# Moving one elementwise product from GpSimd to VectorE in a four-stage kernel whose engines run from hand-ordered tables

## The chip, the cores and the metric

One NeuronCore of one Trainium2 chip runs the whole program. The metric is the device time of one execution in microseconds (us), as the median of several runs. The profile is of one such execution.

## The reference, cut to what matters

The input is 32 images of 128 channels by 32x32 pixels, which is 128 x 1024 numbers per image, in float32. Four blocks follow each other:

```
x = whitening(x)            # 4x4 covariance over all images, Cholesky, one 1x1 mix
x = mamba(x) + x            # per image: norm, W_in, causal conv, silu -> xc ; silu(z)
                            #   delta = softplus(W_dt dt + b)
                            #   h[n] = h[n] * exp(delta * A[n]) + (delta * xc) * B[n]     n = 0..15
                            #   y = sum_n h[n] * C[n] + xc * Dp ; out = W_out (y * silu(z))
x = gamma * attention(x) + x  # 1024 x 1024 softmax per image
x = batchnorm(conv(attention2(x))) + x   # a second 1024 x 1024 softmax per image
```

The change is about the factor `delta * xc` of the recurrence. The kernel calls it `du`.

## The kernel before, in words

The first 150 us or so read all images once for the whitening statistics. The last 110 us or so apply the batch norm. Between them stands the main part: 32 images, each in two chunks of 512 positions (`c` = 0, 1), each chunk in 16 rows (`r`). In row `r` of chunk `c` the kernel does recurrence step `k = 16c + r`, which handles two of the 16 states for one half `h` of the 256 inner channels. So rows 0 to 7 are half 0 and rows 8 to 15 are half 1. The same rows carry pieces of other work: the front of the next chunk (norm, conv, gates, step sizes), and eight tiles of one of the two attentions of an earlier image.

What each engine does within a row, and in which order, is written out in four tables of words (`ORDER_PE`, `ORDER_DVE`, `ORDER_ACT`, `ORDER_POOL`), one string for each of the 16 rows. Each engine runs its own words in that order without overtaking, and waits on semaphores of the others. The words that matter here are these.

- On VectorE (DVE), `dbu` (`spread_inputs`, L554) multiplies the B row by `psU` into PSUM, twice. `scan0` and `scan1` (L567) run the recurrence for the two states into `hs`. `max` (L587) takes the row maximum of an attention tile, `recip` (L581) a reciprocal, and `attend` (L599 and L602, or L606 and L609) scales the attention output. `gate` (L573) forms `y * silu(z)` into `g`, and `normed` (L539) multiplies `xcen` by `rstd`, both in SBUF. `inputs` (L545) copies `du` of the next half into the PSUM bank `psU`.
- On GpSimd (POOL), `prod` (`products`) multiplies `hs` by the C rows (L370), adds the pair of states (L376) and in every second row adds two pairs (L380). In rows of chunk 0 it also copies the last column of the state (L374). `delta0` and `delta1` (`step_size`) finish the step sizes of the next chunk (L356) and multiply them by `xc` into `du` (L361).
- On ScalarE (ACT), `decay` (L752) makes `exp(delta * A)` for the step after, `exp` (L794) the softmax numerators, `copya` and `copyb` (L760) bring transposed tiles out of PSUM, `spread` (L801) the reciprocal sums, and `sp` and `ln` make the softplus parts.
- On TensorE (PE), `energy` makes an attention tile, `turna` and `turnb` transpose it, `weigha` and `weighb` multiply it by the values, `inner0` and `inner1` are the conv products, which wait for `normed`, and `add` sums `prod` results into `psY`.

`hs` has three slots and `pa` four, so VectorE can be at most two steps ahead of GpSimd. The buffer `g` is the same memory as `du`. A max of an attention tile follows its `energy`, the `exp` follows the max, and the next `energy` follows that `exp`.

Of the kernel before, what the change touches and what calls it, by code (L numbers as in the profile page):

```python
# [15 lines left out]
NCH = L // CH  # L16
BCR = 2 * NS
PAIRS = NS // 2
# [13 lines left out]
def build(nc, x, w0, b0, ln_w, ln_b, w_in, conv_w, conv_b, w_x, w_dt, b_dt, a_log, dp, w_out,  # L32
          w_q, b_q, w_k, b_k, w_v, b_v, gam, th_w, ph_w, cv_w, bn_g, bn_b, out):
    fp32, bf16 = mybir.dt.float32, mybir.dt.bfloat16
    ALU = mybir.AluOpType
# [3 lines left out]
    with ctx:  # L39
# [56 lines left out]
        rstd = sb("rstd", [128, CH])  # L96
# [4 lines left out]
        xc = sb("xc", [128, NH, L])  # L101
# [3 lines left out]
        delta = sb("delta", [128, NH, L])  # L105
        du = sb("du", [128, NH, L])
# [45 lines left out]
        S = {}  # L152
# [15 lines left out]
        for k in range(SLOTS):  # L168
# [7 lines left out]
            xi_mm=2 * NCH, xi_ok=2 * NCH, z_mm=2 * NCH, z_ok=2 * NCH, xc_ok=2 * NCH,  # L176
            dbl_mm=NCH, rows_ok=NCH,
            dpre_mm=2 * NCH, sp_abs=2 * NCH, sp_relu=2 * NCH, sp_exp=2 * NCH, sp_ln=2 * NCH,
            delta_ok=2 * NCH, du_ok=2 * NCH,

            u_ok=2 * NCH, dbu_ok=2 * STEPS, da_ok=2 * STEPS, h_ok=2 * STEPS,
            hlast_ok=STEPS // 2, prod=STEPS, pair=STEPS, quad=STEPS // 2, quad_mm=STEPS // 2, g_ok=2 * NCH,
# [9 lines left out]
        def wait(eng, name, b, k):  # L192

            value = b * PER[name] + k
            if isinstance(value, int) and value <= 0:
                return
            eng.wait_ge(S[name], value)

        def at(eng, name, value):
# [33 lines left out]
        ORDER_PE = [  # L233
            "centre variance",
            "energy7 add turna6 weigha2 turnb6",
            "weighb2 resx turna7 residual",
            "turnb7 weigha3 weighb3 query add",
            "",
            "inner0 add inner1",
            "key energy0",  # L240
            "add",
            "values energy1 turna0",
            "gates1 turnb0 skip0 add energy2 gates0",
            "rows turna1 turnb1",
            "energy3 steps0 add",
            "weigha0 steps1 weighb0 turna2 energy4 turnb2 turna3 skip1 turnb3",
            "add",
            "energy5 turna4 weigha1 turnb4 weighb1",
            "turna5 energy6 turnb5 add",
        ]  # L250

        ORDER_DVE = [
            "dbu scan0 scan1 max6",
            "dbu scan0 attend1 scan1 gate1",
            "dbu max7 scan0 scan1",
            "dbu recip3 attend2 scan0 normed scan1",
            "dbu scan0 scan1 attend3",
            "dbu scan0 scan1",
            "dbu scan0 scan1",
            "dbu scan0 inputs scan1 max0",  # L260
            "dbu scan0 scan1 max1",
            "dbu scan0 scan1",
            "dbu scan0 max2 scan1",
            "dbu gate0 scan0 scan1 max3",
            "dbu recip0 scan0 recip1 scan1",
            "dbu scan0 scan1 max4 attend0",
            "dbu scan0 scan1 max5",
            "dbu scan0 inputs recip2 scan1",
        ]

        ORDER_ACT = [
            "decay0 decay1 centre exp6",
            "decay0 spread1 decay1 rstd copya6",
            "exp7 copyb6 spread2 decay0 copya7 decay1",
            "residual copyb7 decay0 spread3 decay1",
            "decay0 decay1",
            "xi0 decay0 decay1 query",
            "decay0 decay1",
            "key decay0 decay1",
            "decay0 xi1 decay1 exp0 value",  # L280
            "decay0 copya0 exp1 decay1 copyb0 silu0 silu1 z1 z0",
            "table decay0 copya1 exp2 decay1 rows",
            "copyb1 decay0 decay1 sp0 exp3",
            "decay0 sp1 decay1 copya2",
            "decay0 ln0 copyb2 decay1 spread0 copya3 exp4",
            "decay0 copyb3 ln1 decay1 copya4 exp5 copyb4",
            "copya5 decay0 decay1 copyb5",
        ]

# [11 lines left out]
            "prod",  # L301
            "prod",
            "prod",
            "prod delta0",
            "prod",
            "prod delta1",
        ]

        def parts(word):
# [12 lines left out]
        def cols(c):  # L322
            return slice(c * CH, (c + 1) * CH)
# [3 lines left out]
        with nc.Block() as block:  # L327


            @block.gpsimd  # L330
            def _(pool):
                n = [0]

                def link(ins):
                    n[0] += 1
                    ins.then_inc(S["consts_made"], 1)
                    pool.wait_ge(S["consts_made"], n[0])

                link(pool.memset(ident[:, :], 0.0))
                link(pool.affine_select(out=ident[:, :], in_=ident[:, :], compare_op=ALU.not_equal, fill=1.0,  # L340
                                        base=0, pattern=[[-1, 128]], channel_multiplier=1))
                link(pool.memset(mask32[:, :], 0.0))
                for q in range(4):
                    link(pool.affine_select(out=mask32[:, :], in_=mask32[:, :], compare_op=ALU.not_equal, fill=1.0,
                                            base=-32 * q, pattern=[[-1, 32]], channel_multiplier=1))
                link(pool.memset(avg[:, :], 1.0 / C))
                link(pool.tensor_tensor(cent[:, :], ident[:, :], avg[:, :], ALU.subtract))
                link(pool.memset(xn[:, 0:KC - 1], 0.0))
                mark["consts"] = n[0]

                def step_size(fb, fc, h):
                    i = 2 * fc + h + 1
                    wait(pool, "sp_relu", fb, i)
                    wait(pool, "sp_ln", fb, i)

                    pool.tensor_tensor(delta[:, h, cols(fc)], delta[:, h, cols(fc)], sp_l[:, h, :], ALU.add  # L356
                                       ).then_inc(S["delta_ok"], 1)
                    wait(pool, "delta_ok", fb, i)
                    wait(pool, "xc_ok", fb, i)
                    wait(pool, "x1_mm", fb - 1, fc + 1)  # L360
                    pool.tensor_tensor(du[:, h, cols(fc)], delta[:, h, cols(fc)], xc[:, h, cols(fc)], ALU.mult  # L361
                                       ).then_inc(S["du_ok"], 1)

                def products(b, k):
                    sl, slot = (b * STEPS + k) % HRING, k % RING
                    h, q = divmod(k % NS, PAIRS)
                    wait(pool, "h_ok", b, 2 * k + 2)
                    wait(pool, "quad_mm", b, k // 2 - 1)
                    at(pool, f"rl{slot}", (b * (STEPS // RING) + k // RING + 1) * 16)
                    pool.tensor_tensor(pa[:, k % PROD, :, :], hs[:, sl, :, :], rows_all[:, slot, 2:4, :], ALU.mult  # L370
                                       ).then_inc(S["prod"], 1)
                    if k < NS:

                        pool.tensor_copy(hlast[:, h, 2 * q:2 * q + 2], hs[:, sl, :, CH - 1]).then_inc(S["hlast_ok"], 1)  # L374
                    wait(pool, "prod", b, k + 1)
                    pool.tensor_tensor(pa[:, k % PROD, 0, :], pa[:, k % PROD, 0, :], pa[:, k % PROD, 1, :], ALU.add  # L376
                                       ).then_inc(S["pair"], 1)
                    if k % 2:
                        wait(pool, "pair", b, k + 1)
                        pool.tensor_tensor(pa[:, k % PROD, 0, :], pa[:, (k - 1) % PROD, 0, :], pa[:, k % PROD, 0, :], ALU.add  # L380
                                           ).then_inc(S["quad"], 1)

                def image(b, scan, more):
                    for c in range(NCH):
                        for r in range(NS):
                            front_of = front_part(b, c, scan, more)
                            for word in ORDER_POOL[r].split():
                                what, n = parts(word)
                                if what == "delta" and front_of:
                                    step_size(*front_of, n)  # L390
                                if what == "prod" and scan:
                                    products(b, NS * c + r)

                for h in range(NH):
                    step_size(0, 0, h)
                image(0, True, True)
                image(1, True, True)
                for b in range(2, NB - 1):
                    image(b, True, True)
                image(NB - 1, True, False)  # L400
# [3 lines left out]
            def _(dve):  # L404
# [135 lines left out]

                def inputs(b, k):
                    ch, h = divmod(k // PAIRS, NH)
                    wait(dve, "du_ok", b, k // PAIRS + 1)
                    wait(dve, "dbu_ok", b, 2 * k)
                    dve.tensor_copy(psU[:, :], du[:, h, cols(ch)]).then_inc(S["u_ok"], 1)  # L545

                def spread_inputs(b, k):
                    slot = k % RING
# [21 lines left out]

                def gate(b, ch, h):
                    wait(dve, "quad_mm", b, (NS * ch + PAIRS * (h + 1)) // 2)
                    dve.tensor_tensor(g[:, h, cols(ch)], psY[:, :], sz[:, h, cols(ch)], ALU.mult  # L573
                                      ).then_inc(S["g_ok"], 1)

# [750 lines left out]
```

## Time and profile before

| | us |
|---|---|
| median of three runs | 5245.92 |
| lowest and highest | 5242.39, 5246.16 |
| the profiled execution, its own time | 5247.66 |
| its span | 5245.8 |

| engine | busy us | share of the span |
|---|---|---|
| PE | 4574.1 | 87% |
| DVE | 4798.9 | 91% |
| ACT | 3722.0 | 71% |
| POOL | 4717.1 | 90% |

1.86 us of the profiled execution lie outside its span. The granted TensorE clock is full in the whole of the main part. Busy shares are means over setup, main part and end. An engine that shows no idle time over an image of the main part can set its period. What the others wait for has to be read in the main part as well.

### The profile page before, as it was taken

The page shows a single profiled execution, that of the slowest core. Times are in us where ns is not written, and L with a number is a line of the kernel's source. Part 1 is how long each engine was busy: PE and PEld are TensorE (multiplying, and loading weights), DVE is VectorE, ACT ScalarE, POOL GpSimd, SP SyncE. Part 2 cuts the span into 40 slices and gives each one's busy share as a digit, 9 for nine tenths or more (in the row PEclk, how much of TensorE's full clock was granted, in tenths as well). Part 3 has the DMA queues.
Part 4 walks back from the last instruction along what each step waited for, and adds up shares of the span by engine and source line. Part 5 has one row for each costly group of instructions (what it writes and reads, how often), then busy time and mean ns, then how long its engine had stood idle before and what let it go on. Part 6 is the DMA issues. An engine that isn't in the chain of part 4 may idle for free.

```text
span 5245.8 us, 62166 instructions
## 1 busy us (share of the span) xinstructions
PE 4574.1 (87%) x17331; PEld 2625.0 (50%) x17331; DVE 4798.9 (91%) x5978; ACT 3722.0 (71%) x6077; POOL 4717.1 (90%) x3342
## 2 busy tenths in 40 slices
PE   7469999999999999999999999999999999999880
PEld 7125555555555555555555555555555555555450
DVE  4689999999999999999999999999999999999933
ACT  3457777777777777777777777777777777777642
POOL 0599999999999999999999999999999999999910
PEclk9679999999999999999999999999999999999995
DMA  4466666666666666666666666666666666666618
GB/s 142 154 237 234 232 243 244 238 236 242 241 232 238 245 241 236 234 249 238 226 241 250 236 236 234 250 238 227 241 248 236 235 241 243 240 230 244 235 73 324
DMA packets 199100, 1216.88 MB, mean 232 GB/s; under 512 B 27880, under 2 KB 28656, under 8 KB 67696
## 3 DMA queue, kind: packets, MB, share of 16 engines
q1 hardware_dynamic: 194416, 1196.26, 62.1%
q10 hardware_dynamic: 4352, 16.78, 0.8%
q8 instruction: 137, 2.24, 0.2%
q14 instruction: 195, 1.60, 0.1%
HBM read 1158.43 MB, written 54.53 MB: 231 GB/s over the span
## 4 chain that ended last, share of the span: by engine, by line
PE 57%; issue 12%; ACT 12%; DVE 12%; POOL 3%; DMA 2%; SPq 0%; DVEq 0%; ACTq 0%; POOLq 0%
PE psT L880 29%; PE psE L880 15%; PE psT L1058 6%; PE psY L880 6%; DVE hs L567 5%; DVE nm L587 3%; ACT da L752 3%; ACT pt L760 2%; ACT p L794 2%; DVE psD L554 2%; POOL pa L370 2%; ACT L722 1%; ACT xc L722 1%; PE psD L880 1%; POOL pa L376 1%
## 5 line engine op out<-in xcount | busy, mean ns | idle before, releaser
L370 POOL TENSOR_TENSOR pa<-hs,rows_all 128x1024 f32<-128x1024 f32 x1024 | 2416.4, 2360 | 8.0 <-DVE hs L567 3.4
L752 ACT ACTIVATE da<-delta,neg_a 128x512 f32<-128x512 f32 x2048 | 1410.0, 715 | 103.7 <-DVE hs L567 85.9
L376 POOL TENSOR_TENSOR pa<-pa 128x512 f32<-128x512 f32 x1024 | 1310.0, 1279 | 40.1
L554 DVE TENSOR_TENSOR psD<-rows_all,psU 128x512 f32<-128x512 f32 x2048 | 1303.0, 681 | 4.8 <-DMA rows_all<-bc_scratch 3.8
L567 DVE TENSOR_TENSOR_SCAN hs<-da,hlast,psD 128x512 f32<-128x512 f32 x1024 | 1266.6, 1263 | 4.0 <-ACT da L752 3.9
L567 DVE TENSOR_TENSOR_SCAN hs<-da,psD 128x512 f32<-128x512 f32 x1024 | 1204.1, 1202 | 2.2 <-POOL hlast L374 1.5
L880 PE MATMUL psT<-pt,va 128*128 128x256 f32 x4096 | 964.2, 381 | 0.0
L760 ACT ACTIVATE pt<-psT 128x512 f32<-128x512 f32 x1024 | 606.3, 592 | 334.9 <-PE psT L1058 332.4
L880 PEld LDWEIGHTS psT<-pt,va 128*128 128x128 f32 x4096 | 746.7, 190 | 161.6 <-issue 76.9
L1058 PEld LDWEIGHTS psT<-ident,p 128*128 128x128 f32 x4096 | 483.7, 141 | 519.0 <-issue 359.7
L794 ACT ACTIVATE p<-psE,nm 128x1024 f32<-128x1024 f32 x512 | 570.1, 1113 | 234.6 <-DVE nm L587 232.6
L587 DVE TENSOR_REDUCE nm<-psE 128x1 f32<-128x1024 f32 x512 | 616.7, 1204 | 126.5 <-PE psE L880 126.4
L1058 PE MATMUL psT<-ident,p 128*128 128x128 f32 x4096 | 630.2, 276 | 106.1 <-ACT pt L760 106.1
L380 POOL TENSOR_TENSOR pa<-pa 128x512 f32<-128x512 f32 x512 | 652.0, 1273 | 40.1
L880 PE MATMUL psY<-pa,ident 128*128 128x512 f32 x1024 | 553.0, 622 | 95.7 <-POOL pa L380 95.0
L880 PE MATMUL psE<-ka,x 128*128 128x512 f32 x1024 | 497.3, 608 | 81.8 <-ACT p L794 42.5
L880 PE MATMUL psE<-ka,qa 128*128 128x512 f32 x1024 | 497.0, 608 | 63.0 <-issue 38.8
L880 PE MATMUL psT<-xn,w_conv 128*128 128x512 f32 x1024 | 468.5, 600 | 4.3 <-DVE xn L539 4.3
L880 PEld LDWEIGHTS psE<-ka,x 128*128 128x128 f32 x1024 | 179.2, 190 | 301.3 <-issue 201.2
L356 POOL TENSOR_TENSOR delta<-delta,sp_l 128x512 f32<-128x512 f32 x128 | 163.0, 1273 | 182.7 <-ACT sp_l L744 182.7
L880 PEld LDWEIGHTS psT<-xn,w_conv 128*128 128x128 f32 x1024 | 197.2, 193 | 257.2 <-issue 249.7
L880 PEld LDWEIGHTS psY<-pa,ident 128*128 128x128 f32 x1024 | 170.8, 193 | 302.4 <-POOL pa L380 155.4
(180 smaller groups left out, 4841.7 us busy)
## 6 DMA issues: line engine op xcount, KB each, us to landing
rows_all<-bc_scratch SPq DMA_DIRECT2D x1024, 1024.0 KB, 4.7
xin<-x SPq DMA_DIRECT2D x40, 512.0 KB, 7.7
xres<-x SPq DMA_DIRECT2D x64, 256.0 KB, 6.1
x_scratch<-x SPq DMA_DIRECT2D x32, 512.0 KB, 5.5
f_scratch<-fa SPq DMA_DIRECT2D x32, 512.0 KB, 6.8
xres<-x SPq DMA_DIRECT2D x8, 512.0 KB, 3.7
x1g<-x SPq DMA_DIRECT2D x8, 512.0 KB, 3.6
fa<-x SPq DMA_DIRECT2D x8, 512.0 KB, 3.7
```

The source lines that it names most:

```text
L356: pool.tensor_tensor(delta[:, h, cols(fc)], delta[:, h, cols(fc)], sp_l[:, h, :], ALU.add).then_inc(S["delta_ok"], 1)
L370: pool.tensor_tensor(pa[:, k % PROD, :, :], hs[:, sl, :, :], rows_all[:, slot, 2:4, :], ALU.mult).then_inc(S["prod"], 1)
L376: pool.tensor_tensor(pa[:, k % PROD, 0, :], pa[:, k % PROD, 0, :], pa[:, k % PROD, 1, :], ALU.add).then_inc(S["pair"], 1)
L380: pool.tensor_tensor(pa[:, k % PROD, 0, :], pa[:, (k - 1) % PROD, 0, :], pa[:, k % PROD, 0, :], ALU.add).then_inc(S["quad"], 1)
L554: dve.tensor_tensor(psD[:, j, :], rows_all[:, slot, j, :], psU[:, :], ALU.mult).then_inc(S["dbu_ok"], 1)
L567: dve.tensor_tensor_scan(hs[:, sl, j, :], da[:, k % 2, j, :], psD[:, j, :], hlast[:, h, n_:n_ + 1] if ch else 0.0, ALU.mult, ALU.add).then ...
L587: dve.tensor_reduce(nm[:, i % 2:i % 2 + 1], flat(psE), AX, ALU.max, negate=True).then_inc(S["nm_ok"], 1)
L752: act.activation(da[:, k % 2, j, :], delta[:, h, cols(ch)], ACT.Exp, scale=neg_a[:, h, 2 * q + j:2 * q + j + 1]).then_inc(S["da_ok"], 1)
L760: act.activation(pt[:, i // GT % 2, 4 * q:4 * q + 4, 128 * (t % GT):128 * (t % GT) + 128], psT[:, 0, :].rearrange("p (j i) -> p j i", j=4) ...
L794: act.activation(p[:, i % 2, :], flat(psE), ACT.Exp, bias=nm[:, i % 2:i % 2 + 1], accum_out=rsum[:, i % (2 * GT):i % (2 * GT) + 1]).then_i ...
L880: return pe.matmul(dst, lhsT, rhs, start=start, stop=stop)
L1058: last = pe.transpose(psT[:, 0, 128 * j:128 * j + 128], p[:, i % 2, (4 * q + j) * 128:(4 * q + j + 1) * 128], ident[:, :])
```

## The change

GpSimd no longer makes `du`. VectorE's `inputs`, which was a copy of `du` into `psU`, becomes a multiplication of `delta` by `xc` with its result in `psU`. It waits for `delta_ok` and `xc_ok` instead of `du_ok`. Because `g` lies in the memory of `du`, `gate` takes over the wait on `x1_mm` of the previous image. The four order tables are new: on GpSimd, `delta0` and `delta1` now stand together after the `prod` of row 13, and on the other three engines many words are moved by a place or a row.

```
                 def step_size(fb, fc, h):
...
-                    wait(pool, "delta_ok", fb, i)
-                    wait(pool, "xc_ok", fb, i)
-                    wait(pool, "x1_mm", fb - 1, fc + 1)
-                    pool.tensor_tensor(du[:, h, cols(fc)], delta[:, h, cols(fc)], xc[:, h, cols(fc)], ALU.mult
-                                       ).then_inc(S["du_ok"], 1)
...
                 def inputs(b, k):
                     ch, h = divmod(k // PAIRS, NH)
-                    wait(dve, "du_ok", b, k // PAIRS + 1)
+                    wait(dve, "delta_ok", b, k // PAIRS + 1)
+                    wait(dve, "xc_ok", b, k // PAIRS + 1)
                     wait(dve, "dbu_ok", b, 2 * k)
-                    dve.tensor_copy(psU[:, :], du[:, h, cols(ch)]).then_inc(S["u_ok"], 1)
+                    dve.tensor_tensor(psU[:, :], delta[:, h, cols(ch)], xc[:, h, cols(ch)], ALU.mult
+                                      ).then_inc(S["u_ok"], 1)
...
                 def gate(b, ch, h):
                     wait(dve, "quad_mm", b, (NS * ch + PAIRS * (h + 1)) // 2)
+                    wait(dve, "x1_mm", b - 1, ch + 1)
```

The new tables, rows 0 to 15 (before, `ORDER_DVE` had `gate1` in row 1, `normed` in row 3, `inputs` between the scans of row 7, and `max4 attend0` at the end of row 13):

```
ORDER_DVE                                   ORDER_PE
 0 dbu scan0 scan1 max6                      centre variance
 1 dbu scan0 attend1 scan1                   energy7 add turna6 weigha2 turnb6
 2 max7 dbu gate1 scan0 scan1                weighb2 turna7 resx residual turnb7
 3 dbu scan0 recip3 attend2 scan1            weigha3 weighb3 query add
 4 dbu scan0 scan1 attend3
 5 normed dbu scan0 scan1                    inner0 key inner1 add energy0
 6 dbu scan0 scan1
 7 dbu scan0 scan1 inputs max0               values add
 8 dbu scan0 scan1 max1                      energy1 turna0
 9 dbu scan0 scan1                           turnb0 gates1 skip0 gates0 energy2 turna1 add
10 dbu scan0 max2 recip0 scan1               rows turnb1
11 dbu scan0 scan1                           energy3 steps0 weigha0 steps1 add weighb0
12 gate0 dbu max3 scan0 scan1                turna2 energy4 turnb2 turna3 turnb3 skip1
13 dbu scan0 scan1 recip1 max4               energy5 weigha1 turna4 add
14 dbu attend0 scan0 scan1                   turnb4 weighb1
15 dbu max5 scan0 inputs recip2 scan1        turna5 energy6 turnb5 add
```

ACT in the new rows 13 and 14: `ln0 copyb2 decay0 spread0 copya3 decay1 exp4`, then `decay0 ln1 copyb3 copya4 decay1 exp5 copyb4`. POOL: `prod` in each row, and in row 13 `prod delta0 delta1` (before: `prod delta0` in row 13 and `prod delta1` in row 15).

## Rows read from the trace of the kernel before

**Rows 1.** Part 1 of the page: busy time, share, instructions.
```profile
PE 4574.1 (87%) x17331; PEld 2625.0 (50%) x17331; DVE 4798.9 (91%) x5978; ACT 3722.0 (71%) x6077; POOL 4717.1 (90%) x3342
```

**Rows 2.** The chain that ended last, same piece of chunk: start us, us, what.
```profile
390.76 5.15 PE psT L880 x22
...
4901.02 5.15 PE psT L880 x22
```

**Rows 3.** Timeline of POOL: start us, us, engine, line, operation.
```profile
2069.44 1.28 POOL L356 TENSOR_TENSOR delta<-delta,sp_l 128x512 f32<-128x512 f32 x1
2070.80 1.28 POOL L361 TENSOR_TENSOR du<-delta,xc 128x512 f32<-128x512 f32 x1
2072.03 2.37 POOL L370 TENSOR_TENSOR pa<-hs,rows_all 128x1024 f32<-128x1024 f32 x1
2074.48 1.27 POOL L376 TENSOR_TENSOR pa<-pa 128x512 f32<-128x512 f32 x1
2075.71 2.37 POOL L370 TENSOR_TENSOR pa<-hs,rows_all 128x1024 f32<-128x1024 f32 x1
...
2080.73 2.36 POOL L370 TENSOR_TENSOR pa<-hs,rows_all 128x1024 f32<-128x1024 f32 x1
2083.17 1.59 POOL L376 TENSOR_TENSOR pa<-pa 128x512 f32<-128x512 f32 x1
2084.91 2.36 POOL L370 TENSOR_TENSOR pa<-hs,rows_all 128x1024 f32<-128x1024 f32 x1
```

**Rows 4.** Waits of DVE, one image (2044.64 to 2194.99): total, times, longest.
```profile
DVE nm L587 <- PE psE L880: 1.9, 3, 1.1
DVE psT L599 <- ACT rb L801: 0.9, 1, 0.9
```

**Rows 5.** Timeline of DVE in the same stretch as POOL's.
```profile
2062.50 1.20 DVE L567 TENSOR_TENSOR_SCAN hs<-da,psD 128x512 f32<-128x512 f32 x1
2063.61 1.26 DVE L554 TENSOR_TENSOR psD<-rows_all,psU 128x512 f32<-128x512 f32 x2
2064.79 2.44 DVE L567 TENSOR_TENSOR_SCAN hs<-da,hlast,psD 128x512 f32<-128x512 f32 x2
2067.15 1.20 DVE L587 TENSOR_REDUCE nm<-psE 128x1 f32<-128x1024 f32 x1
2068.27 1.28 DVE L554 TENSOR_TENSOR psD<-rows_all,psU 128x512 f32<-128x512 f32 x2
...
2070.65 0.46 DVE L599 SCALAR_TENSOR_TENSOR psT<-psT,cvec,rb 128x256 f32<-128x256 f32 x1
...
2071.49 1.27 DVE L567 TENSOR_TENSOR_SCAN hs<-da,hlast,psD 128x512 f32<-128x512 f32 x1
...
2081.23 2.41 DVE L539 TENSOR_TENSOR xn<-xcen,rstd 128x512 f32<-128x512 f32 x1
2083.57 1.27 DVE L567 TENSOR_TENSOR_SCAN hs<-da,hlast,psD 128x512 f32<-128x512 f32 x1
```

**Rows 6.** All instructions of line 539: ns min/median/max, first and last start.
```profile
L539 DVE TENSOR_TENSOR xn<-xcen,rstd x64: 693/2413/2685, 162.2 to 4862.4; 128x512 f32<-128x512 f32 x64
```

**Rows 7.** Timeline of DVE, second chunk of the first image.
```profile
274.80 1.75 DVE L539 TENSOR_TENSOR xn<-xcen,rstd 128x512 f32<-128x512 f32 x1
276.48 1.27 DVE L567 TENSOR_TENSOR_SCAN hs<-da,hlast,psD 128x512 f32<-128x512 f32 x1
```

**Rows 8.** The chain of work in the main part: start us, us, what.
```profile
2040.55 1.98 PE psE L880 x4
...
2084.68 0.38 ACT rb L801
...
2105.03 1.21 DVE nm L587
...
2115.99 1.99 PE psE L880 x4
...
2162.68 3.44 PE psT L880 x8
```

More of the change, by code:

```diff
@@ L178, in build @@
             dpre_mm=2 * NCH, sp_abs=2 * NCH, sp_relu=2 * NCH, sp_exp=2 * NCH, sp_ln=2 * NCH,
-            delta_ok=2 * NCH, du_ok=2 * NCH,
+            delta_ok=2 * NCH,
             u_ok=2 * NCH, dbu_ok=2 * STEPS, da_ok=2 * STEPS, h_ok=2 * STEPS,
@@ L235, in build @@
             "energy7 add turna6 weigha2 turnb6",
-            "weighb2 resx turna7 residual",
-            "turnb7 weigha3 weighb3 query add",
-            "",
[L239 to L248, printed above, removed]
+            "weighb2 turna7 resx residual turnb7",
+            "weigha3 weighb3 query add",
+            "",
+            "inner0 key inner1 add energy0",
+            "",
+            "values add",
+            "energy1 turna0",
+            "turnb0 gates1 skip0 gates0 energy2 turna1 add",
+            "rows turnb1",
+            "energy3 steps0 weigha0 steps1 add weighb0",
+            "turna2 energy4 turnb2 turna3 turnb3 skip1",
+            "energy5 weigha1 turna4 add",
+            "turnb4 weighb1",
             "turna5 energy6 turnb5 add",
@@ L253, in build @@
             "dbu scan0 scan1 max6",
-            "dbu scan0 attend1 scan1 gate1",
-            "dbu max7 scan0 scan1",
-            "dbu recip3 attend2 scan0 normed scan1",
+            "dbu scan0 attend1 scan1",
+            "max7 dbu gate1 scan0 scan1",
+            "dbu scan0 recip3 attend2 scan1",
             "dbu scan0 scan1 attend3",
+            "normed dbu scan0 scan1",
             "dbu scan0 scan1",
-            "dbu scan0 scan1",
-            "dbu scan0 inputs scan1 max0",
+            "dbu scan0 scan1 inputs max0",
             "dbu scan0 scan1 max1",
             "dbu scan0 scan1",
[L263 to L268, printed above, removed]
+            "dbu scan0 max2 recip0 scan1",
+            "dbu scan0 scan1",
+            "gate0 dbu max3 scan0 scan1",
+            "dbu scan0 scan1 recip1 max4",
+            "dbu attend0 scan0 scan1",
+            "dbu max5 scan0 inputs recip2 scan1",
         ]
@@ L272, in build @@
             "decay0 decay1 centre exp6",
-            "decay0 spread1 decay1 rstd copya6",
-            "exp7 copyb6 spread2 decay0 copya7 decay1",
-            "residual copyb7 decay0 spread3 decay1",
+            "spread1 rstd decay0 copya6 exp7 decay1",
+            "decay0 decay1 copyb6 copya7",
+            "decay0 decay1 spread2 residual copyb7 spread3",
+            "decay0 query decay1",
             "decay0 decay1",
-            "xi0 decay0 decay1 query",
-            "decay0 decay1",
+            "xi0 decay0 decay1",
             "key decay0 decay1",
[L280 to L286, printed above, removed]
+            "decay0 xi1 exp0 decay1 value",
+            "decay0 decay1 copya0 exp1 copyb0 silu0 silu1 z1 z0",
+            "table copya1 decay0 exp2 rows decay1 copyb1",
+            "decay0 decay1 sp0",
+            "decay0 sp1 decay1 exp3 copya2",
+            "ln0 copyb2 decay0 spread0 copya3 decay1 exp4",
+            "decay0 ln1 copyb3 copya4 decay1 exp5 copyb4",
             "copya5 decay0 decay1 copyb5",
@@ L303, in build @@
             "prod",
-            "prod delta0",
+            "prod delta0 delta1",
             "prod",
-            "prod delta1",
+            "prod",
         ]
```

## The prediction

> **What bounds the kernel now.** I read the page's busy shares first: three engines stand at 87 to 91% [rows 1], so no share names the bound. The chain of work gives the beat: the same piece of a chunk comes at 390.76 and 60 chunks later at 4901.02 [rows 2], which is 75.17 us per chunk and 150.34 us per image over 30 images. Then the timelines. On POOL the reader is to see that each instruction starts as the one before it ends [rows 3], and over a whole image the list of waits has no row for POOL. A pair of rows of `prod` takes 80.73 - 72.03 = 8.70 us, of which the even row is 75.71 - 72.03 = 3.68 and the odd one 5.02. A `delta` with its `du` takes 72.03 - 69.44 = 2.59. An image then costs 16 x 8.70 + 4 x 2.59 = 149.6, and two stalls of about 0.5 (below) bring it to 150.6: that is the beat, so POOL is full. VectorE is nearly full. Its waits over one image are 1.9 for `psE` and twice 0.9 for `rb` (the second, for L606, repeats the row shown) [rows 4], so 3.7 of 150.34. A chain through PE is as long as the chunk too: PE owns most of the pieces between `energy3` at 2040.55 and the end of `weighb3` at 2084.68 [rows 8].
>
> **What the collision costs.** `normed` is the only instruction of the main part that reads two SBUF tensors on VectorE. It takes 693 ns at its shortest, but 2413 at the median of 64 [rows 6]. In the timeline it is issued at 2081.23, while `prod` runs since 2080.73, and the next instruction starts at 2083.57 [rows 3, 5]. So it got through at 2083.57 - 0.61 = 2082.96, 2.2 us after the start of that `prod`, where `prod` ends. The 0.61 is the 693 ns less the 0.08 by which neighbours overlap. Its price is 2.34 instead of 0.61, 1.73 us. POOL loses too: the step from L376 to the next `prod` is 84.91 - 83.17 = 1.74 instead of 75.71 - 74.48 = 1.23, 0.5 us more. Once `normed` costs only 276.48 - 274.80 = 1.68, 1.07 over its own time [rows 7]. The price is thus not fixed; it is what is left of the POOL instruction that is running, from 0 to 2.2 after the start of a `prod` and 0 to 1.1 after that of a short one. Instructions with one SBUF input and one in PSUM show none of it: `dbu` takes 0.59 each [rows 5].
>
> The Trainium skill (SBUF — State Buffer, "Who interferes with whom") says that a VectorE instruction with two SBUF inputs contends with a GpSimd instruction that reads SBUF, and the later one blocks wholly. By that rule the trace agrees (2413 against 693 ns), and the rule speaks against this change, because it names the inputs and not the output.
>
> **The change part by part.**
>
> *POOL loses `du`.* Four times an image 2.59 becomes the 1.23 of one short operation. That is 4 x 1.36 = 5.4, to 144.2, and with stalls of 0.5 at six collisions 147.2 at most. Moving `delta1` up beside `delta0` adds nothing to POOL, but puts `prod` of row 14 later by 1.23 while VectorE has two steps of room.
>
> *VectorE's `inputs`.* The copy becomes a product of `delta` and `xc`, both in SBUF, into PSUM. No row shows two SBUF inputs with a PSUM output. The bounds are 0 extra (as `dbu`, which writes PSUM) and 1.73 extra (the median of `normed`) for each, four times an image. I take the mechanism of `normed`, because it is nearest in what it reads, with the time that its place gives.
>
> *Where each collision falls.* VectorE without its waits and the two collisions costs 150.34 - 3.7 - 2 x 1.73 = 143.1. I laid the new rows of both engines side by side: on VectorE the `dbu` pair 1.18, `scan` 1.12 in chunk 0 and 1.18 in chunk 1, `max` 1.12, `attend` 0.84 [rows 5], the gates and `inputs` 0.6 without collision, as one `dbu`; on POOL 3.68, 5.02 and 1.23 [rows 3], and `prod` 0.15 after the end of `scan1` at the earliest. Take the end of `scan1` of row 13 in chunk 1 as zero. `inputs` of row 15 is issued at 0.07 + 1.12 (`max4`) + 1.18 + 0.8 + 2.36 (row 14) + 1.18 + 1.12 + 1.18 = 9.0. POOL has the `prod`, two short ones and both deltas of row 13, 7.5 us, then `prod` of row 14. In the steady beat it comes 1.0 behind, so this `prod` starts at 8.6 and lets `inputs` through at 10.8: 1.8 us. Going on in the same way I get 0.9 for `normed` in chunk 0 (behind the last addition of row 3), 0.6 for `inputs` of row 7 (1.6 into `prod` of row 6), 0.4 for row 15 of chunk 0 (behind `delta1`), 0.4 for `normed` in chunk 1 and 1.6 for row 7 of chunk 1. The sum is 5.7 for six collisions, 0.95 each, against 3.5 for two now. VectorE comes to 143.1 + 5.7 = 148.8 without waits.
>
> *The waits that are left.* `attend0` moves behind the next `dbu`, which gives `rb` 1.18 more, and `spread0` stands earlier on ACT: its 0.9 goes. `max4` in row 13 stays near the end of `energy4`. The new tight place is `normed`, now in row 5 straight behind `attend3` and straight ahead of `inner0`. The PE chain: from `energy3` to the end of `weighb3` it was 2084.68 - 2040.55 = 44.1 [rows 8]. Then come `spread3` (0.38), `attend3` (0.84) and the way between engines, 1.4 in all, `normed` 0.6 plus its collision, and from `inner0` to `energy0` 26 matmuls of 3.44 / 8 = 0.43, 11.2 [rows 8], with the way to `max0` 11.5. From `max0` to `max1` it is 4.6, and from `max1` to `energy3` 115.99 - 105.03 = 11.0 [rows 8]. The sum is 73.2 plus the collision, near 74. VectorE's 148.8 is 74.4 per chunk, so the two meet often. For two loops this close I estimate 0.9 us of waits per image (one wait of rows 4 instead of four). That gives 149.7.
>
> *The rest.* The wait on `x1_mm` in `gate` is for a product of the image before, done long before row 12. The new `delta_ok` and `xc_ok` are met: `delta0` ends near 3 where `inputs` needs it at 9. SP's transfers keep their order; nothing is loaded or stored anew. In the setup and the first image, where VectorE waits for `du`, three paths get shorter by one 1.3 us product: 4 us.
>
> **The sum.** 30 x (149.7 - 150.34) = -19, and -4: 5247.7 - 23 = 5225 for the profiled execution. That one is 1.7 above the median of the runs, so I say 5223.
>
> **The rivals.**
>
> *The normed chain becomes the bound* (slower). `normed` now lies on PE's path; before, `add` and earlier work covered it. For it: the 60 executions of the main part cost 1.73 over their own time at the median [rows 6]. Then the chain is 74.2 + 1.7 = 75.9 per chunk (with 1.0 for `energy3` to `weighb3` being longer by ACT's new order), 151.8 per image, 30 x 1.5 = +44: 5290. Against it: the walk puts it behind a short addition. It decides from a collision of about 1 us at this one place.
>
> *All six collisions cost the full 1.73* (slower). 143.1 + 10.4 + 0.9 = 154.4, 30 x 4.1 = +122: 5364. The sum turns from gain to loss at a mean of (150.34 - 143.1 - 0.9) / 6 = 1.06 each, only 0.1 above my 0.95. Against it: with VectorE behind, POOL idles at times and starts fresh after `scan1`.
>
> *The output in PSUM spares `inputs` the collision* (faster). Then 143.1 + 2 x 0.95 + 1.5 of waits is 146.5, PE's chain holds it near 147.5: 30 x -2.8 - 4 = -88, 5158.
>
> *No difference that shows.* Gain and collisions cancel, within 10 us of before. The three engines' loops are all within 1 us per chunk of each other, which is why it has weight.
>
> **How the numbers follow.** Forecast (5190 to 5235) 0.42; `inputs` spared 0.12; nothing 0.14; the `normed` chain 0.22; full price 0.10. A measurement of this kernel tells about 0.2% (10 us) from no change. So faster is 0.54, the same 0.14, slower 0.32. The range leaves out the full price and the far side of the spared case: 5155 to 5305. Cases of both signs hold much of it; the likeliest one's own range is 5190 to 5235.
>
> **What the profile after would show.** POOL has idle time in front of L370 waiting for `hs`, and its beat no longer equals its work. `inputs` is a TENSOR_TENSOR of clearly more than 0.69 us at the median, near 1.6, with values that differ between rows 7 and 15. `normed` has a median near 1.3 instead of 2.4. VectorE's waits fall to about 1 us per image. The prediction is wrong if `inputs` takes 0.69 throughout, if `normed` stays at 2.4, or if the waits for `psE` and `rb` grow instead of shrinking.

## The result: 1.2% slower

The changed kernel takes 5308.5 us at the median (5305.0 to 5313.7, four runs) against 5246.0 (5242.4 to 5247.9, four runs) of the kernel before. The ratio is 1.012, with a 95% interval of 1.0107 to 1.0133. I had forecast 5223 and a range of 5155 to 5305, so the sign was wrong, and the time lies just outside the range.

The page of the changed kernel, parts 1 and 5 (busy and mean ns of one, then idle before and its releaser). VectorE's busy time went up by 70 us where GpSimd's went down by 128 [rows 1]. GpSimd, which waited for nobody over an image before, now has 190 us of idle time ahead of its `prod`, put down to `hs`:

```profile
PE 4580.0 (86%) x17331; PEld 2615.9 (49%) x17331; DVE 4868.8 (92%) x5978; ACT 3685.5 (69%) x6077; POOL 4589.2 (87%) x3214
...
L365 POOL TENSOR_TENSOR pa<-hs,rows_all 128x1024 f32<-128x1024 f32 x1024 | 2443.1, 2386 | 206.2 <-DVE hs L564 190.1
```

The beat, from the chain of work of the changed kernel (start us, us, what). It is 152.5 us per image instead of 150.34 [rows 2], and 30 times 2.16 is 65 us, which covers the whole loss of 62.5:

```profile
2251.63 4.18 PE psT L878 x20
...
2404.16 4.18 PE psT L878 x20
...
2556.66 4.18 PE psT L878 x20
```

All instructions of the two lines that read two SBUF tensors on VectorE: the product of `inputs` (L541) and `normed` (L534), min/median/max in ns. The collision is there with a PSUM output too: 668 ns at the shortest and 2706 at the longest. Its median of 1634 is the time of almost no execution: of the 128, 62 take under 1.1 us and 59 over 2.4. `normed` fell to 1326 from 2413 [rows 6]:

```profile
L541 DVE TENSOR_TENSOR psU<-delta,xc x128: 668/1634/2706, 187.0 to 5014.5; 128x512 f32<-128x512 f32 x128
...
L534 DVE TENSOR_TENSOR xn<-xcen,rstd x64: 668/1326/1697, 161.7 to 4926.2; 128x512 f32<-128x512 f32 x64
```

The timeline of VectorE over one image, the six instructions concerned. In row 7 `inputs` takes 2.70 us (chunk 1) and 2.62 (chunk 0), 2.0 and 1.9 above its own time. In row 15 it takes 0.67:

```profile
2257.17 1.27 DVE L534 TENSOR_TENSOR xn<-xcen,rstd 128x512 f32<-128x512 f32 x1
2258.36 1.28 DVE L551 TENSOR_TENSOR psD<-rows_all,psU 128x512 f32<-128x512 f32 x2
...
2268.99 2.70 DVE L541 TENSOR_TENSOR psU<-delta,xc 128x512 f32<-128x512 f32 x1
2271.60 1.21 DVE L585 TENSOR_REDUCE nm<-psE 128x1 f32<-128x1024 f32 x1
...
2276.34 1.20 DVE L585 TENSOR_REDUCE nm<-psE 128x1 f32<-128x1024 f32 x1
...
2307.09 0.67 DVE L541 TENSOR_TENSOR psU<-delta,xc 128x512 f32<-128x512 f32 x1
...
2333.28 1.56 DVE L534 TENSOR_TENSOR xn<-xcen,rstd 128x512 f32<-128x512 f32 x1
2334.77 1.28 DVE L551 TENSOR_TENSOR psD<-rows_all,psU 128x512 f32<-128x512 f32 x2
...
2345.04 2.62 DVE L541 TENSOR_TENSOR psU<-delta,xc 128x512 f32<-128x512 f32 x1
2347.57 1.21 DVE L585 TENSOR_REDUCE nm<-psE 128x1 f32<-128x1024 f32 x1
...
2382.72 0.68 DVE L541 TENSOR_TENSOR psU<-delta,xc 128x512 f32<-128x512 f32 x1
```

GpSimd and then PE in the stretch of the first of them. GpSimd ends its addition of row 5 (L375) at 2267.1, then idles 1.65 us, and starts the `prod` of row 6 at 2268.79, 0.2 us ahead of `inputs`. The profile puts this wait down to `hs`, but `scan1` of row 6 had ended at 2265.45. What ends at the right moment is PE's `add` at 2267.55 + 1.10. `products` waits for `quad_mm`, because `pa` has four slots. So the `prod` of row 6 may not start before the `add` of rows 2 and 3, and the new PE table has that `add` in row 5 behind `inner1`. The old table had it ahead of `inner1`.

```profile
2262.07 2.36 POOL L365 TENSOR_TENSOR pa<-hs,rows_all 128x1024 f32<-128x1024 f32 x1
2264.51 1.27 POOL L371 TENSOR_TENSOR pa<-pa 128x512 f32<-128x512 f32 x1
2265.86 1.27 POOL L375 TENSOR_TENSOR pa<-pa 128x512 f32<-128x512 f32 x1
2268.79 2.35 POOL L365 TENSOR_TENSOR pa<-hs,rows_all 128x1024 f32<-128x1024 f32 x1 [1.65 <-DVE hs L564]
2271.21 1.60 POOL L371 TENSOR_TENSOR pa<-pa 128x512 f32<-128x512 f32 x1
```

```profile
2265.69 1.88 PE L878 MATMUL psT<-xn,w_conv 128*128 128x512 f32 x4
2267.41 0.28 PE L878 MATMUL psT<-edge,ident 128*128 128x3 f32 x2
2267.55 1.10 PE L878 MATMUL psY<-pa,ident 128*128 128x512 f32 x2
2268.49 1.88 PE L878 MATMUL psE<-ka,x 128*128 128x512 f32 x4
```

VectorE's waits over one image of the changed kernel (total, times, longest). They sum to 3.6 us, about as much as before [rows 4], but the largest is new: `recip2` of row 15 stands behind the `exp` of the tile whose `max5` now comes in the same row.

```profile
DVE rinv L579 <- ACT p L792: 2.2, 2, 1.2
DVE nm L585 <- PE psE L878: 0.4, 1, 0.4
DVE hs L564 <- ACT da L750: 0.4, 1, 0.4
DVE hs L564 <- issue: 0.3, 1, 0.3
DVE fa L604 <- ACT rb L799: 0.3, 1, 0.3
```

### The profile page after: what moved, and what is told of

Same layout as the page of the kernel before. It is cut to its first block, busy times and chain, and to the rows that moved or that the text cites. A ratio compares the mean times of both kernels' runs of the same rounds, so it can differ in the third digit from the quotient of the medians.

```text
span 5303.2 us, 62035 instructions
## 1 busy us (share of the span) xinstructions
PE 4580.0 (86%) x17331; PEld 2615.9 (49%) x17331; DVE 4868.8 (92%) x5978; ACT 3685.5 (69%) x6077; POOL 4589.2 (87%) x3214
## 4 chain that ended last, share of the span: by engine, by line
PE 62%; DVE 13%; issue 10%; ACT 10%; POOL 3%; DMA 2%; DVEq 0%; SPq 0%; ACTq 0%; POOLq 0%
PE psT L878 29%; PE psE L878 18%; PE psT L1056 8%; PE psY L878 6%; DVE hs L564 5%; ACT da L750 3%; ACT p L792 3%; DVE psD L551 2%; DVE nm L585 2%; POOL pa L365 2%; DVE psU L541 2%; PE psD L878 1%; POOL pa L371 1%; DMA rows_all<-x_scratch 1%; ACT pt L758 1%
## 5 line engine op out<-in xcount | busy, mean ns | idle before, releaser
L365 POOL TENSOR_TENSOR pa<-hs,rows_all 128x1024 f32<-128x1024 f32 x1024 | 2443.1, 2386 | 206.2 <-DVE hs L564 190.1
L750 ACT ACTIVATE da<-delta,neg_a 128x512 f32<-128x512 f32 x2048 | 1394.1, 714 | 141.7 <-DVE hs L564 119.4
L1056 PEld LDWEIGHTS psT<-ident,p 128*128 128x128 f32 x4096 | 472.6, 141 | 561.3 <-issue 350.3
L375 POOL TENSOR_TENSOR pa<-pa 128x512 f32<-128x512 f32 x512 | 650.8, 1271 | 40.1
L878 PEld LDWEIGHTS psE<-ka,qa 128*128 128x128 f32 x1024 | 179.0, 190 | 277.7 <-issue 154.9
```

The lines of the kernel that those rows point to most:

```text
L750: act.activation(da[:, k % 2, j, :], delta[:, h, cols(ch)], ACT.Exp, scale=neg_a[:, h, 2 * q + j:2 * q + j + 1]).then_inc(S["da_ok"], 1)
L878: return pe.matmul(dst, lhsT, rhs, start=start, stop=stop)
L1056: last = pe.transpose(psT[:, 0, 128 * j:128 * j + 128], p[:, i % 2, (4 * q + j) * 128:(4 * q + j + 1) * 128], ident[:, :])
```

## The experiments

The first reading left two theories. Theory C says that the collision of `inputs` in row 7 costs the time, because it stands ahead of `max0`. Theory O says that the new order costs it. All times are medians; "beat" is the time per image in the main part.

**E1: a copy in place of the product.** The factor `xc` is left out of the recurrence's input here.

```
-                    dve.tensor_tensor(psU[:, :], delta[:, h, cols(ch)], xc[:, h, cols(ch)], ALU.mult
-                                      ).then_inc(S["u_ok"], 1)
+                    dve.tensor_copy(psU[:, :], delta[:, h, cols(ch)]).then_inc(S["u_ok"], 1)
```

> The changed kernel, but VectorE copies delta into psU instead of multiplying delta by xc (the factor xc is left out of the recurrence's input). Everything else, tables and waits included, is that of the changed kernel. If the product's collision with GpSimd is the cause (theory C): inputs falls to 0.67 us, max0 then waits for energy0 only, which was ready 1.3 us earlier per chunk, so 152.5 - 2.5 = 150.0 us per image and 5308 - 75 = 5233 us. If the new order of the tables is the cause (theory O): the time stays within 10 us of 5308.

Measured: 5233.4 us (5227.3 to 5237.5), 0.998 of the kernel before (0.9968 to 0.9991). The collision costs 75 us, and theory C gave the number. `max0` now waits 0.7 us for `energy0`, so of the 4 us per image that VectorE saves, 2.4 show (beat 150.1).

**E2: the old tables with the product.** Only the four `ORDER_` tables are put back.

> The product on VectorE, with the four old order tables. Theory C: the collision comes along, at a place between scan0 and scan1; with a mean of 1 to 1.7 us each, VectorE has 143.1 + 3.5 + 4 to 7 + up to 3.7 of waits, 151 to 156 us per image, 5270 to 5400 us. Theory O: without the new tables the saving on GpSimd shows, 147 to 149 us per image, 5150 to 5210 us.

Measured: 5271.9 us (5268.3 to 5282.3), ratio 1.0058 (1.0041 to 1.0075), beat 151.2 on average (150.75 in most images, 151.7 or more in about one of four). The product costs with the old order too: the same tables with a copy in its place take 5222 (E9). One of two executions in row 7 is hit, between the scans, where a `prod` began 0.16 us before it:

```profile
2330.53 2.35 POOL L365 TENSOR_TENSOR pa<-hs,rows_all 128x1024 f32<-128x1024 f32 x1
```

```profile
2330.69 2.75 DVE L541 TENSOR_TENSOR psU<-delta,xc 128x512 f32<-128x512 f32 x1
2333.36 1.21 DVE L564 TENSOR_TENSOR_SCAN hs<-da,psD 128x512 f32<-128x512 f32 x1
```

**E3: the new tables with the old product.** The kernel before, with the four tables of the changed one.

> The kernel before with the four new order tables: GpSimd makes du, VectorE copies it. Theory C: no collision of inputs; GpSimd is full again at about 150.3 us per image and has both delta and both du in one block of 5.2 us, so 5235 to 5265 us. Theory O: the tables cost by themselves, 5300 us or more.

Measured: 5272.2 us (5270.4 to 5275.1), ratio 1.0054 (1.0037 to 1.007). That is between the two expectations. The tables cost 26 us where GpSimd still makes `du`. In its trace both deltas and both `du` stand in one block of 5.2 us, and over one image VectorE waits 1.8 us there for `du` and 0.7 for the `exp`. That these waits are the 26 us was not tested.

**E4: `recip2` behind `scan1`.** DVE row 15: `dbu max5 scan0 inputs scan1 recip2`.

> The changed kernel with recip2 of row 15 behind scan1 instead of ahead of it, so that scan1 no longer stands behind the exp of tile 5. Theory C: VectorE's 1.0 and 1.2 us of waiting there go, but the chain runs through PE in that stretch, so the time stays within 10 us of 5308. If VectorE's own queue is the bound, 2.2 us per image are won: 5308 - 66 = 5242 us.

Measured: 5307.7 us (5303.8 to 5308.6), the time of the changed kernel. But the 2.2 us of waiting did not go, as I had expected; they moved. VectorE now waits for the `decay0` of the next row, 1.5 us in each chunk, and `decay0` stands on ScalarE behind transposed tiles that come from TensorE:

```profile
2307.95 1.27 DVE L551 TENSOR_TENSOR psD<-rows_all,psU 128x512 f32<-128x512 f32 x2
2310.68 2.33 DVE L564 TENSOR_TENSOR_SCAN hs<-da,psD 128x512 f32<-128x512 f32 x2 [1.46 <-ACT da L750]
```

So VectorE is held in that stretch from outside, whichever of its words comes first. The bound there is not VectorE's queue.

**E5: the copy in row 7 only.** `xc` is left out for these halves.

```
+                    if h == 1:
+                        dve.tensor_copy(psU[:, :], delta[:, h, cols(ch)]).then_inc(S["u_ok"], 1)
+                        return
```

> The changed kernel with the copy of delta instead of the product only for inputs of row 7 (xc is left out there); row 15 keeps the product. If row 7's collision (2.0 us each, twice per image) is the whole price, this is the copy in both places again: 5225 to 5243 us. If row 15's product or the waits of recip2 share in it: 5255 or more.

Measured: 5233.0 us (5231.4 to 5237.7), the same as E1. The collision of row 7 is the whole of E1's gain. Row 15's product on VectorE is free, also with the 0.4 us by which it is hit in one chunk of two here.

**E6: one word of PE's table moved.** Row 5 of `ORDER_PE`: `inner0 add key inner1 energy0` instead of `inner0 key inner1 add energy0`.

> The changed kernel with PE's add of row 5 behind inner0 instead of behind inner1. Theory H: the prod of row 6 is held back by that add (its pa slot is free only after it) and so starts 0.2 us ahead of inputs. Then it starts about 1.5 us earlier, the wait of inputs falls from 2.0 to 0.3 to 0.7 us, and most of 2.5 us per image is won: 5235 to 5255 us. If prod of row 6 starts where it does because of the scans: inputs stays at 2.6 us and the time at 5308.

Measured: 5240.9 us (5239.1 to 5245.0), ratio 0.999 (0.9981 to 1.0), beat 150.1. The move of one word on another engine takes back 68 us. In its timeline the `prod` of row 6 starts straight behind the addition, 1.9 us ahead of `inputs`, which finds it nearly done and takes 1.00 us (1.28 in the other chunk). `max0` then waits 0.41 for `energy0`:

```profile
2240.36 1.27 POOL L375 TENSOR_TENSOR pa<-pa 128x512 f32<-128x512 f32 x1
2241.59 2.35 POOL L365 TENSOR_TENSOR pa<-hs,rows_all 128x1024 f32<-128x1024 f32 x1
2244.02 1.59 POOL L371 TENSOR_TENSOR pa<-pa 128x512 f32<-128x512 f32 x1
```

```profile
2243.50 1.00 DVE L541 TENSOR_TENSOR psU<-delta,xc 128x512 f32<-128x512 f32 x1
2244.91 1.23 DVE L585 TENSOR_REDUCE nm<-psE 128x1 f32<-128x1024 f32 x1 [0.41 <-PE psE L878]
```

**E7: `inputs` ahead of both scans.** DVE row 7: `dbu inputs scan0 scan1 max0`.

> The changed kernel with inputs of row 7 straight behind dbu, ahead of both scans (DVE row 7: dbu inputs scan0 scan1 max0). It is then issued near the end of a short POOL instruction while the next prod is still held: a wait of about 0.5 us instead of 2.0. If the price is the phase of this collision: 1.3 us per chunk won, 5230 to 5245 us. If a product on VectorE costs by itself wherever it stands: within 15 us of 5308.

Measured: 5246.7 us (5245.1 to 5251.9), ratio 1.0004 (0.9995 to 1.0014). The product's mean is 0.83 us in the main part instead of 1.65, and 62 us come back. It is 2 us above the upper end of what I expected. The stretch up to `max0` is as short as in E6, so the wait of `inputs` for the `dbu` just ahead of it (7.3 us in sum) does not show there. In chunk 0 the way from `max0` to `max1` is longer, 4.82 us instead of 4.58. The trace says through whom: with `inputs` ahead of it `scan0` comes later, so ScalarE's `decay0` waits longer for `hs`, `xi1` (L716) stands behind it, and TensorE's `values`, which stand ahead of `energy1`, wait for `xi1`:

```profile
2621.54 0.72 ACT L750 ACTIVATE da<-delta,neg_a 128x512 f32<-128x512 f32 x1 [2.32 <-DVE hs L564]
2622.17 0.67 ACT L716 ACTIVATE xc<-psT,cbias 128x512 f32<-128x512 f32 x1
```

```profile
2622.89 2.05 PE L878 MATMUL psT<-w_v_t,x 128*128 128x128 f32 x16 [0.18 <-ACT xc L716]
```

**E8: E6 and E7 together.**

> Both edits: add behind inner0 and inputs of row 7 ahead of the scans. If both only remove the same 2.0 us collision, it is no better than the better one of the two: 5225 to 5245 us, with max0 bound by energy0. If the held prod also costs by itself, 10 us or more below both.

Measured: 5250.3 us (5247.5 to 5251.3), ratio 1.0007 (0.9998 to 1.0017). Both edits remove the same 2 us, and together they are no better than E7 alone. But it is 5 us above the range that I expected and 9 above E6: the longer way from `max0` to `max1` of E7 is in its trace too (4.82), and nothing is won for it.

**E9: the old tables with the copy.** E1's edit with the old tables (`xc` left out).

> The four old tables, and VectorE copies delta into psU (xc is left out), so GpSimd has no du to make and inputs does not collide. It shows what the freed 5.4 us per image on GpSimd are worth with the old order. If GpSimd alone was the bound before: 147 to 149 us per image, 5145 to 5210 us. If the chain through PE and VectorE was as long: 5225 us or more.

Measured: 5222.2 us (5221.7 to 5224.8), ratio 0.9958 (0.9943 to 0.9973), beat 149.7. GpSimd, freed of all four `du`, now has 5.0 us of waits per image, and yet only 24 us are won. That is between the two expectations and close to the second. GpSimd was full before, but the chain through PE and VectorE was nearly as long, 0.6 us per image shorter.

**E10: the old tables, `inputs` ahead of both scans.** DVE row 7: `dbu inputs scan0 scan1 max0` in the old table.

> The four old tables with the product on VectorE, and inputs of row 7 ahead of both scans instead of between them. With the old place one of its two executions per image waited 2.1 us (issued 0.16 us after a prod). Moved by 1.1 us it falls on the short addition before: about 1 us. If phases decide: 0.5 to 1.1 us per image better than the 5272 of the old place, 5238 to 5258 us. If the product costs the same everywhere: 5272.

Measured: 5296.2 us (5290.2 to 5297.9), ratio 1.0094 (1.0078 to 1.0109). The expectation failed. The execution that had waited 2.1 us takes 1.38 now, but the one of the other chunk, which had taken 0.67, takes 1.52. Moving the product off one GpSimd instruction put the other onto one. In sum the two are 0.5 us per image cheaper than in E2, but each now also starts 0.2 us late, behind the `dbu` that it waits for, and the two products of row 15 take 0.93 and 1.00 where they took 0.67 and 0.99. So nothing is won on VectorE. Why the kernel is 24 us slower stays open.

**E11: `add` ahead of `inner0`.** Row 5 of `ORDER_PE`: `add inner0 key inner1 energy0`, in the gap in which PE waits for `normed`.

> The changed kernel with add of row 5 ahead of inner0, in the 1.8 and 0.5 us in which PE waits for normed. The prod of row 6 is free at least as early as with add behind inner0, and the path from normed to energy0 is 0.86 us shorter; max0 waited 0.4 us for it in one chunk of two, so up to 0.4 us per image better than add behind inner0: 5226 to 5241 us. If VectorE's queue is the bound in that stretch: 5241 us.

Measured: 5225.6 us (5222.2 to 5227.7), ratio 0.9963 (0.995 to 0.9977), beat 149.5. This is the changed kernel with one word of a table moved, and it beats both: 0.4% below the kernel before, 1.6% below the changed one.

**E12: E11 with `normed` ahead of `attend3`.** DVE row 4: `dbu scan0 scan1 normed attend3`.

> The same with normed ahead of attend3 on VectorE (DVE row 4: dbu scan0 scan1 normed attend3), so that inner0 starts about 0.8 us earlier. VectorE's queue up to max0 is no shorter, so no gain over add first (within 10 us) unless normed's own collision gets smaller; 5215 to 5241 us. If the chain through PE still bounds: 1 us per image better, near 5205 us.

Measured: 5232.1 us (5230.6 to 5234.2), ratio 0.9976 (0.9966 to 0.9985). `normed` got cheaper (0.94 us at the mean instead of 1.42), but `inputs` of row 7 got dearer by moving with the queue: 1.29 and 1.71 instead of 1.01 and 1.28. The collision moved.

With the two kernels, four of the runs make a table. The product's price depends on the order (50 us with the old tables, 75 with the new), and the order's on the product. In each of the three pairs the new tables are the slower ones. The two runs with 5222 and 5233 leave out the factor `xc`:

| | `inputs` is a copy of what is there | `inputs` is the product |
|---|---|---|
| old tables, GpSimd makes `du` | 5246 | |
| old tables, no `du` on GpSimd | 5222 | 5272 |
| new tables, GpSimd makes `du` | 5272 | |
| new tables, no `du` on GpSimd | 5233 | 5308 |

## Why the prediction was wrong

**What bounds.** That GpSimd was full was right (it has no waits over an image), and freeing it of `du` with nothing put in its place is worth 24 us (E9). That the other loops lie within 1 us of GpSimd's fits this too. "The only instruction that reads two SBUF tensors" was too wide: the scans of chunk 1 read `da` and one column of `hlast`. But all 1024 of them take 1.24 to 1.28 us in the kernel before, so that column draws them into no collision.

**The mechanism of the collision** was right: a product with two SBUF inputs waits for the GpSimd instruction that is running, with a PSUM output as well. The rival in which the output spares it fell. The sum was right as well: I had 5.7 us for six collisions and the trace has 2.0 + 1.9 + 0.6 + 0.9 = 5.4. So the time VectorE spends in them came out well sized. For `normed` that was the walk (0.9 and 0.4 forecast, 0.9 and 0.6 measured). For `inputs` it was luck: its four terms were off in both directions and cancelled.

**Where each collision falls, and on which path,** is the step that failed. I had 1.8 and 0.4 for row 15, and it measured nothing. I had 0.6 (chunk 0) and 1.6 (chunk 1) for row 7, and it measured 1.9 and 2.0. My walk laid only two engines side by side, and let the `prod` of row 6 start when GpSimd was free and `hs` was there. I left out that `products` also waits for `quad_mm`, hence for a word of PE's table that this change moves. E6 shows it: with that `add` earlier, the same product in the same place takes 1.00 in place of 2.70.

**The PE chain** is where this became time. I added `normed`'s collision to it but not that of `inputs`, since I took 11.5 us of matmuls from `normed` to `max0`. In the trace VectorE's own queue is longer than those matmuls there. Even with my places for the collisions it would have been 11.5 and 12.8 (the measured 12.8 and 13.2, less 1.9 and 2.0, plus 0.6 and 1.6), an estimate of 1.3 us per image that I had left out; the wrong places are the other 1.7. The table cuts one turn of the chain into five pieces, for the changed kernel, E6 and E11, each from its timelines in the middle of the main part (for the changed kernel from the rows above, from `energy3`, at 2286.73 and 2362.52, and from the `rb` of `spread3`, at 2255.83 and 2331.89):

| piece of the chain, us | forecast, per chunk | changed kernel, chunks 1 and 0 | E6 (E1 is the same) | E11 |
|---|---|---|---|---|
| end of `normed` to `max0` | 11.5 | 13.2, 12.8 | 12.0, 11.6 | 11.6, 11.5 |
| `max0` to `max1` | 4.6 | 4.7, 4.6 | 4.7, 4.6 | 4.7, 4.6 |
| `max1` to `energy3` | 11.0 | 10.4, 10.4 | 10.4, 10.4 | 10.4, 10.4 |
| `energy3` to the end of `weighb3` | 44.1 | 45.2, 45.8 | 45.2, 45.8 | 45.2, 45.8 |
| `spread3`, `attend3`, `normed` | 2.0 and its collision | 2.9, 2.5 | 2.9, 2.5 | 2.9, 2.5 |
| sum | 73.2 and the collision | 152.5 for both | 150.1 | 149.5 |

That each sum is the beat proves nothing, since the pieces fill one turn. What shows that this chain bounds is that only the first line moves when the collision of row 7 goes or shrinks, and that the beat moves by as much. The first line was 1.3 to 1.7 us longer than forecast. The fourth line was 1.1 to 1.7 longer than before; it belongs to the new order and not to the collision, since it stays in E1, E6 and E11 and is 44.1 to 44.5 in E9 with the old tables. `max1` to `energy3` gives 0.6 per chunk back. Without the collision's 2.4 us the time would have been 5233 (E1), inside the range of my likeliest case, so the fourth line alone would not have failed the forecast. Which words of the new tables make it longer was not tested.

**The waits that are left** I had at 0.9, and they are 3.6. The largest, 2.2 for `recip2`, does not go when that word is moved (E4); it turns into a wait for `decay0`. Adding VectorE's waits to its work (143.2 + 5.4 + 3.6 = 152.2; my 143.1 was rounded wrongly) nearly gives the beat, but says nothing of the cause, because those waits are what the chain through PE leaves.

**The signs I had named.** GpSimd does wait for `hs`, `normed` did fall to 1.3, and `inputs` has its median at 1.6. That match is luck: the median lies in the gap between executions of 0.67 and of 2.6. None of the three signs of being wrong came: the waits for `psE` and `rb` shrank from 3.7 us in the image read before to 0.7. A bound that moves to another instruction shows in none of them; the beat would have been the sign to name.

**The rivals.** The `normed` chain (5290) was nearest: the bound is that chain, and the price is a collision in it. But the collision is not `normed`'s, which cost 0.6 and 0.9. The full price for all six fell, and so did no difference.

The Trainium skill (SBUF — State Buffer, "Who interferes with whom") says that the order of issue decides who blocks. By that rule the trace agrees: `inputs` issued 0.2 us after a `prod` waits 2.0 us, and GpSimd's addition, issued behind the waiting product, loses 0.33 (1.60 against 1.27).

## What to carry to other kernels

In these runs a VectorE product of two SBUF tensors costs what is left of the GpSimd instruction that runs when it is issued, from 0 to 2.1 us beside GpSimd products of 2.36 and additions of 1.27. So its price belongs to its place, and a place is set by every engine that can hold GpSimd back, also through a buffer that TensorE frees. When walking a new order by hand, take each wait of each instruction, not the two engines that seem to matter. A sum of stalls over one engine can come out right, as the 5.7 us did, while what counts is the one stall ahead of the instruction that feeds the longest chain. Before giving up a change that loses, move the words around its worst stall: here one word on a third engine turned 1.2% slower into 0.4% faster.

## What the runs showed of the hardware

The waiting product gets through at the end of the running GpSimd instruction, ahead of the next, even where these follow each other without a gap. In E10 it was issued at 2341.80 during an addition begun at 2341.35, and took 1.38 us. The `prod` behind, which shows a start at 2342.58, took 2.81 us instead of 2.35. Without a collision it takes 0.67 us from SBUF and SBUF into PSUM, the time of the copy that it replaced. The profile put GpSimd's wait for TensorE's `add` down to VectorE's `hs`, since of several waits it names one by the time of its event; an idle time of 1.65 us that began when that `hs` had been there for 1.7 was the sign.
